# Deferred shared down products, last routers in one run, grouped last stage, expert word kept over the branch

## What is computed

```python
x = layernorm(x + attn(x))              # 16 heads, sqrt-distance bias; 2048 tokens of 256
xf = x.reshape(2048, 256)
scores = sigmoid(xf @ gate_w.T)         # 32 experts in 8 groups, the 4 best groups, the 6 best experts of those
w, idx = top6(mask_groups(scores)); w = w / w.sum() * 2.5
y = sum over the 6 picks: w * ((silu(xf @ w11[e].T) * (xf @ w33[e].T)) @ w22[e].T)
shared = (silu(xf @ sw1.T) * (xf @ sw3.T)) @ sw2.T
out = layernorm(x + y + shared)
```

## Time and profile before

| | us |
|---|---|
| median of 3 runs (lowest, highest) | 565.51 (562.99, 566.81) |
| the profiled execution | 565.8 |
| its span in the trace | 564.0 |
| busy of that span: PE, DVE, ACT, POOL | 459.8, 378.2, 321.9, 226.4 |

### The profile page before, as it was taken

The page is one execution under the profiler, slowest core; times in us unless marked ns, Lnnn a source line. Parts: engine busy times, 40 slices in busy tenths (PEclk is TensorE's granted clock), DMA queues, the critical chain, the costliest instruction groups (busy, mean ns, idle before and its releaser), DMA issues.

```text
span 564.0 us, 12967 instructions
## 1 busy us (share of the span) xinstructions
PE 459.8 (82%) x3190; PEld 377.7 (67%) x3191; DVE 378.2 (67%) x1745; ACT 321.9 (57%) x1093; POOL 226.4 (40%) x244
## 2 busy tenths in 40 slices
PE   4366779797968787767997999999999999992972
PEld 3254557575756555534556999898989898991761
DVE  4036385969697878974636677776767777772696
ACT  1059698878888979814102555555555555552133
POOL 0000000070716253477550657656566666563000
PEclk9669898889999989989999999999999999997897
DMA  4569659896978833289953555545455555523992
GB/s 130 125 221 269 153 139 267 228 273 164 242 170 234 203 103 102 77 307 416 416 198 82 168 153 166 160 145 168 139 154 158 156 160 158 143 63 121 420 409 95
DMA packets 67996, 107.92 MB, mean 191 GB/s; under 512 B 9189, under 2 KB 55018, under 8 KB 66416
## 3 DMA queue, kind: packets, MB, share of 16 engines
q1 hardware_dynamic: 54016, 75.15, 46.5%
q0 software_dynamic: 10752, 26.13, 14.0%
q10 hardware_dynamic: 3184, 6.13, 2.9%
HBM read 64.03 MB, written 43.33 MB: 190 GB/s over the span
## 4 chain that ended last, share of the span: by engine, by line
PE 55%; DVE 19%; DMA 10%; ACT 8%; issue 5%; SPq 2%; DVEq 0%; POOLq 0%; ACTq 0%; POOL 0%
PE bank L698 21%; PE bank L707 11%; DVE s_neg L980 5%; PE bank L688 5%; PE bank L637 5%; ACT probs L800 5%; DMA k_scratch<-k_lo 3%; PE bank L478 3%; DMA k_pack<-k_scratch 3%; PE bank L646 2%; PE bank L541 2%; ACT pT L811 2%; DMA xt<-xT 1%; DMA x1T_all<-x1T 1%; DVE ey_all L1339 1%
## 5 line engine op out<-in xcount | busy, mean ns | idle before, releaser
L1383 POOL DMA_INDIRECT routed<-rows,position x96 | 93.5, 974 | 194.5 <-DVE position L1144 166.9
L1393 POOL DMA_INDIRECT expert_out<-ey_all,out_row x128 | 130.1, 1017 | 93.4 <-issue 64.0
L800 ACT ACTIVATE probs<-s_neg,m_neg 128x128 f32<-128x128 f32 (+1 forms) x256 | 114.1, 450 | 38.1 <-DVE m_neg L980 37.9
L980 DVE CUSTOM_DVE_ANT_0 s_neg<-bank,bias_sb 128x128 f32<-128x128 f32 (+1 forms) x256 | 79.6, 351 | 54.7 <-PE bank L510 53.5
L898 ACT ACTIVATE eg<-bank 128x128 f32<-128x128 f32 x128 | 35.6, 278 | 88.9 <-PE bank L698 88.3
L707 PE MATMUL bank<-expert_w,ea 128*128 x256 | 78.8, 390 | 1.7 <-DVE ea L1296 0.6
L698 PEld LDWEIGHTS bank<-xgT,xn 128*128 128x128 f32 x512 | 66.5, 191 | 9.2 <-issue 5.6
L698 PE MATMUL bank<-xgT,xn 128*128 128x128 f32 x512 | 68.1, 276 | 3.6 <-issue 3.0
L510 PE MATMUL bank<-k_pack,q_pack 128*128 128x256 f32 (+1 forms) x128 | 58.3, 464 | 15.2 <-DMA k_pack<-k_scratch 12.6
L905 ACT ACTIVATE ey_all<-bank,pick 128x256 f32<-128x256 f32 x128 | 60.0, 469 | 1.8 <-DVE out_row L1309 1.5
L811 ACT ACTIVATE pT<-bank 128x512 f32<-128x512 f32 x96 | 55.8, 583 | 0.0
(11 more groups left out here) (160 smaller groups left out, 812.2 us busy)
## 6 DMA issues: line engine op xcount, KB each, us to landing
xg<-routed SPq DMA_DIRECT2D x128, 137.5 KB, 2.1
expert_w<-expert_out SPq DMA_DIRECT2D x16, 768.0 KB, 14.4
expert_w<-expert_weights SPq DMA_DIRECT2D x9, 1024.0 KB, 17.7
q_pack<-q_scratch SPq DMA_DIRECT2D x32, 256.0 KB, 5.0
routed<-empty SPq DMA_DIRECT2D x8, 550.0 KB, 12.8
k_pack<-k_scratch SPq DMA_DIRECT2D x16, 256.0 KB, 7.1
expert_w<-expert_weights ACTq DMA_DIRECT2D x3, 1024.0 KB, 13.5
xt<-xT SPq DMA_DIRECT2D x9, 256.0 KB, 7.8
```

What stands on the lines that cost most here:

```text
L800: act.activation(probs[g % 2][qb][:, 2 * pair + r, :], s_neg[u][:, r, 0:n], ACT.Exp, bias=m_neg[:, u, r:r + 1], scale=-1.0, accum_out=row_ ...
L980: dve.tensor_tensor_reduce(out=s_neg[u][:, r, 0:n], in0=SCORES[u][:, n * r:n * r + n], in1=bias_sb[:, REP * g + 2 * pair + r, SEQ - n:SEQ] ...
L1383: pool.indirect_dma_start(routed, bass.IndirectOffsetOnAxis(ap=position[b % ROW_BUFS][:, t, j:j + 1], axis=0), rows[b % ROW_BUFS][:, t, :] ...
L1393: pool.indirect_dma_start(expert_out, bass.IndirectOffsetOnAxis(ap=out_row[:, k:k + 1], axis=0), ey[k], None, bounds_check=TOKENS * TOPK - ...
```

## The change

The tiles of the shared down product are split in two. Eight (`SH_NOW`) are done in the transition as before. The other eight (`SH_LAST`) are done after the slot loop, straight into the eight PSUM banks, together with their `x_sum` tile; for this `sh_a` keeps all four blocks. The last stage works in groups of 4, 4, 4, 2 and 2 tiles: ten tiles are summed by TensorE and six by VectorE, and the small steps (root, polish, scale) are done once per group. In the transition the pieces of the routers of batches 6 and 7 stand in one run on VectorE, between them the layer norm of batch 7 and little else; TensorE does `shared_up` of the first block ahead of `ranks` of batch 6. The copies of batch 7 (`keep_x1`) go out from ScalarE's queue, ahead of its `gate_exps`, and not from SP's. SP waits for the tables first, reads two of them, and only then waits for the scatters. In the slot loop TensorE reads a word of `packed_tab` one slot after its first use before, and carries it over the loop's branch in a register (`word_back`). Several tiles take the place of others (`xgT` in `x1T`, `ey` in `rows`, `y_three` in `xg`).

```diff
...
-F_STATS = 9
 F_DEEP = 4
+F_GROUPS = ((0, 4), (4, 8), (8, 12), (12, 14), (14, 16))
+F_SUMMED = (0, 2, 4, 5, 7, 9, 10, 12, 13, 15)
+F_ADDED = tuple(t for t in range(TILES) if t not in F_SUMMED)
+SH_LAST = F_SUMMED[:8]
+SH_NOW = tuple(t for t in range(TILES) if t not in SH_LAST)
...
-        sh_a = [sb(f"sh_a{m}", [P, 512]) for m in range(2)]
+        sh_a = sb("sh_a", [P, 4, 2, 512])
...
-        xgT = [sb(f"xgT{i}", [P, KC, P], F32, late) for i in range(4)]
+        xg_all = sb("xg_all", [P, UNROLL, ROW], F32, late)
...
+        xgT = [x1T_flat[i // 2][:, DIM * (i % 2):DIM * (i % 2) + DIM].rearrange("p (c t) -> p c t", c=KC)
+               for i in range(4)]
...
-        ey_all = sb("ey_all", [P, UNROLL * DIM], F32, late)
-        ey = [ey_all[:, DIM * k:DIM * k + DIM] for k in range(UNROLL)]
+        ey = [rows[k // 2][:, k % 2, 0:DIM] for k in range(UNROLL)]
...
+        def f_source(t):
+            if t in F_SUMMED:
+                return bank[F_SUMMED.index(t) % 8][:, 0:DIM]
+            return f_resid[F_ADDED.index(t) % F_DEEP]
...
             load_weights(sp, 0)
             load_weights(sp, 1)
-            keep_x1(BATCH - 1, 1)
             load_weights(sp, 2)
             sp.wait_ge(pads_written, 16 * (BATCH + 1))
+            sp.wait_ge(fin_step, FIN_STEPS + 3)
+            def row_of(s):
+                return sp.value_load(slot_tab[0:1, bass.ds(s, 1)], min_val=0, max_val=EXPERTS * REGION)
+            early_rows = [row_of(k) for k in range(2)]
             for i in range(2):
                 sp.wait_ge(scattered[i], 16 * 2 * TOPK * BATCH // 2)
-            sp.wait_ge(fin_step, FIN_STEPS + 3)
...
             def load_slot(s, k, turn):
-                at = sp.value_load(slot_tab[0:1, bass.ds(s, 1)], min_val=0, max_val=EXPERTS * REGION)
+                at = early_rows[k] if turn is None and k < len(early_rows) else row_of(s)
                 if turn is not None:
                     sp.wait_ge(ey_ready[k], turn)
-                sp.dma_start(xg[k][:], routed[bass.ds(at, P), :]).then_inc(rows_loaded[k], 16)
...
             def shared_down(tb):
                 pe.wait_ge(sh_act, 2 * tb + 2)
-                for t in range(4):
-                    need(pe, sh_added, 4 * tb + t - 1)
-                    for m in range(2):
-                        last = pe.matmul(DOWN[t % 2][:, 0:DIM], sh_a[m][:, P * t:P * t + P],
-                                         sw2_sb[:, m, :], start=(m == 0), stop=(m == 1))
-                    last.then_inc(sh_down, 1)
+                for t in SH_NOW:
+                    if t // 4 == tb:
+                        n = SH_NOW.index(t)
+                        need(pe, sh_added, n - 1)
+                        down_tile(t, DOWN[n % 2][:, 0:DIM], True).then_inc(sh_down, 1)
...
             last_b = BATCH - 1
             values(last_b, 1, 1)
             project_out(last_b, 1)
-            ranks(last_b - 1, 0)
             shared_up(0, 0)
             shared_up(0, 1)
+            ranks(last_b - 1, 0)
             turn_x1(last_b, 1)
+            gate(last_b, 1)
             shared_up(1, 0)
-            gate(last_b, 1)
-            shared_down(0)
             shared_up(1, 1)
             ranks(last_b, 1)
             shared_up(2, 0)
...
             shared_up(2, 1)
-            shared_down(1)
+            shared_down(0)
+            shared_up(3, 0)
...
-            shared_up(3, 0)
             shared_up(3, 1)
+            shared_down(1)
             shared_down(2)
             shared_down(3)
             pe.wait_ge(fin_step, FIN_STEPS + 3)
-            pe.wait_ge(sh_added, TILES)
+            pe.wait_ge(sh_added, len(SH_NOW))
...
             def step(k, turn):
                 if k == 0 and turn.opens:
                     held.clear()
+                    if not turn.first:
+                        held["word"] = pe.snap(word_back, min_val=0, max_val=EXPERTS ** PACKED - 1)
                 if k == 0 and isinstance(turn.turn, int) and turn.turn < W_GROUPS - 1:
                     pe.wait_ge(late_loaded[turn.turn], 16 * W_PARTS)
-                now = None
                 if turn.exists(k, 0):
-                    now = held.pop("next") if "next" in held else expert_of(turn, k)
                     gate_up(k, turn)
-                following = turn if k < UNROLL - 1 and turn.slot is None else turn.next
-                if following is not None and turn.exists(k, 1):
-                    held["next"] = expert_of(following, (k + 1) % UNROLL)
+                if turn.exists(k, -1):
+                    if (k - 1) % PACKED == 0:
+                        held["word"] = experts_of(turn.turn * (UNROLL // PACKED) + (k - 1) // PACKED)
+                    last = expert_in(held["word"], k - 1)
                 if turn.exists(k, 2):
                     turn_rows(k, turn, 2)
                 if turn.exists(k, -1):
-                    last = held.get("last")
-                    if last is None:
-                        last = expert_in(experts_of(turn.turn * (UNROLL // PACKED) - 1), k - 1)
                     down(k, turn, last)
-                held["last"] = now
+                if k == UNROLL - 1 and turn.slot is None and turn.next is None:
+                    pe.reg_mov(word_back, held["word"])
...
+            for i in (0, 1, 6, 7, 2, 3, 4, 5):
+                t = SH_LAST[i]
+                if i == 2:
+                    for k in range(UNROLL - 4, UNROLL):
+                        pe.wait_ge(ey_ready[k], SLOTS // UNROLL)
+                down_tile(t, f_source(t), False)
+                pe.matmul(f_source(t), ident, x_sum[:, t, :], start=False, stop=False)
+            for n, t in enumerate(F_SUMMED):
+                to = f_source(t)
+                if n >= 8:
+                    pe.wait_ge(f_done, F_SUMMED[n - 8] + 1)
+                    pe.matmul(to, ident, x_sum[:, t, :], start=True, stop=False)
                 pe.wait_ge(rows_loaded[t % UNROLL], y_in(t))
-                need(pe, f_done, 2 * (p - F_DEEP + 1))
                 for j in range(TOPK):
-                    pe.matmul(to, ident, rows_y[:, t, DIM * j:DIM * j + DIM], start=(j == 0), stop=False)
-                pe.matmul(to, ident, x_sum[:, t, :], start=False, stop=True).then_inc(f_summed, 1)
+                    last = pe.matmul(to, ident, rows_y[:, t, DIM * j:DIM * j + DIM], start=False,
+                                     stop=(j == TOPK - 1))
+                last.then_inc(f_summed, 1)
...
             shared_silu(0, 0)
             shared_silu(0, 1)
             copy_x1t(last_b, 1, last_b // 2)
-            shared_silu(1, 0)
+            act.wait_ge(x1t_copied, BATCH)
+            act.dma_start(x1T_all[:, :, last_b * SEQ:BATCH * SEQ], x1T[1][:]).then_inc(x1_kept[1], 16)
+            act.dma_start(x_sum[:, 2 * last_b:2 * BATCH, :], x1[last_b % ROW_BUFS]).then_inc(x1_kept[1], 16)
             gate_exps(last_b)
             load_weights(act, W_GROUPS - 1)
-            shared_silu(1, 1)
-            for tb in (2, 3):
+            for tb in (1, 2, 3):
                 for m in range(2):
                     shared_silu(tb, m)
...
+            def final_apply(g):
+                act.wait_ge(f_fin, 5 * g + 5)
+                for i, t in enumerate(range(*F_GROUPS[g])):
+                    pair, at = t // 2, t // 2 % F_DEEP
+                    need(act, out_stored[at], 16 * (pair // F_DEEP))
+                    act.activation(f_out[at][:, t % 2, :], f_source(t), ACT.Identity,
+                                   scale=f_small[:, g % 2, 6, i:i + 1],
+                                   bias=f_small[:, g % 2, 7, i:i + 1]).then_inc(f_done, 1)
+                    if t % 2 == 1:
+                        act.wait_ge(f_done, t + 1)
+                        act.dma_start(out_t[t - 1:t + 1].rearrange("t p d -> p t d"), f_out[at]
+                                      ).then_inc(out_stored[at], 16)
...
+            for g, (a, z) in enumerate(F_GROUPS):
+                cols = f_small[:, g % 2, :, 0:z - a]
+                act.wait_ge(f_stat, f_stats_by(g))
+                act.activation(cols[:, 1, :], cols[:, 0, :], ACT.Ln).then_inc(f_root, 1)
+                act.wait_ge(f_root, 2 * g + 1)
+                act.activation(cols[:, 2, :], cols[:, 1, :], ACT.Exp, scale=-0.5).then_inc(f_root, 1)
+                if g > 0:
+                    final_apply(g - 1)
+            final_apply(len(F_GROUPS) - 1)
...
-                need(dve, sh_down, 4 * tb)
-                dve.tensor_tensor(sh_a[m][:], T_BANK[m][:], sh_g[m][:], ALU.mult).then_inc(sh_act, 1)
+                dve.tensor_tensor(sh_a[:, tb, m, :], T_BANK[m][:], sh_g[m][:], ALU.mult).then_inc(sh_act, 1)
...
             b = BATCH - 1
+            router_piece(b - 1, 0, 0)
             norm(b, 1, 1)
-            for part in range(4):
-                router(b - 1, 0, part)
+            for piece in range(1, 6):
+                router_piece(b - 1, 0, piece)
             ln_stats(b, 1, b // 2)
             ln_moments(b)
+            for piece in range(6, 10):
```

(51 more changed lines are left out.)

91 lines of the change are left out of this document (31 added, 60 removed).

## The result

The changed kernel took 550.08 us (median of 4 runs, 545.41 to 553.8) against 564.5 us (562.99 to 566.81) beside it: ratio 0.9702, 95% interval 0.9658 to 0.9747. The ratio leaves out the run of 553.8 us, which counts as slow (over 1.5% above the fastest), so it isn't the quotient of the two medians. A second measurement on another chip gave 548.12 against 565.43, ratio 0.9701 (0.9645 to 0.9758). Forecast: 550.0, between 545 and 557, faster.

A forecast was written before the change was run, and what follows sets the result against it. TensorE was taken to bound the loop, with scatters and TensorE's shared products setting its start; 564.0 - 10.1 + 1.7 - 4.7 - 2.7 = 548.2 us of span, with 1.8 around it 550.0, range 545 to 557.

The forecast's parts named there:

- What bounds the kernel: Loop start: scatters with row loads and TensorE's shared products end close together; relieving TensorE alone gains 5.6 us at most.
- Which part does it: Transition: deferring eight down tiles takes 7.4 us from TensorE, the new order brings scatters sooner; gain 10.1 us.
- Router and scatters: Transition: batch 7's `position` comes at about 265 us, so GpSimd needn't wait and issues its last scatter at 286.5.
- The lag: Last scatter's issue to SP's first row load: 3.98 us, less 0.6 for the table read moved ahead of the wait.
- rival 2: Scatters fall 2.6 us behind beside two weight queues; loop starts at 294.6, time 552.6 us; chance 0.12.
- The copies: Transition: batch 7's copies, issued 18 us before `shared_up(3, 0)` needs them, cost nothing.
- The clock: Loop start: after 6 us idle TensorE restarts at about half clock, costing 1.7 us; bounds 0 and 1.7.
- The branch: Slot loop: taking both table reads out of the gap at the branch gains 4.7 us; bounds 1.8 and 6.1.
- Rival 1: Slot loop: the branch itself keeps its price, gain only 1.8 us, time 552.9 us; chance 0.12.
- The last stage: After the loop: row transfer sets the floor, the last store comes 2.7 us sooner; bounds 0 and 4.5.
- rival 3: The last stage gains nothing; time 552.7 us; chance 0.09.
- rival 4: Last stage: TensorE's clock falls to 1.2 GHz throughout, making its added work slower; time 586.6 us; chance 0.04.

The follow-up runs named there:

- experiment 4: Changed kernel with order of routers and shared products as before and no down products deferred; rest kept: 560.73 us, ratio 0.9900.
- experiment 3: Changed kernel with the order of routers and shared products as before, eight down products still deferred: 547.74 us, ratio 0.9718.
- experiment 2: Changed kernel with all sixteen shared down products done in the transition, nothing deferred, new order kept: 544.27 us, ratio 0.9677.
- experiment 7: Changed kernel with the last 3 MB of weights sent by ScalarE behind the first two slots' copies in the loop: 548.48 us, ratio 0.9715.
- experiment 5: Changed kernel with fourteen products that nothing reads added on TensorE behind the last shared product, ahead of the loop: 546.37 us, ratio 0.9720.
- experiment 8: Changed kernel with the copies of batch 7 issued by SP between its weight transfers, not by ScalarE: 547.0 us, ratio 0.9722.
- experiment 1: Changed kernel with TensorE's two table reads returned to where the kernel before has them, at the loop's branch: 553.16 us, ratio 0.9837.
- experiment 10: Changed kernel with the last 3 MB of weights sent from SP behind its first eight row loads, four down products deferred: 557.37 us, ratio 0.9875.

## Why the prediction was right, point by point

- **What bounds the kernel.** It named two chains that end close together, TensorE's products and the scatters, and put 5.6 us on relieving TensorE alone. The runs bear out the picture and not that bound: the deferral alone took the transition from 61.87 (experiment 4) to 54.46 (experiment 3), 7.4 us, since it brings `position` 2.9 us sooner as well. The two chains aren't independent, because `shared_add` stood among the pieces of the router.
- **Which part does it.** Here the working was wrong without hurting the sum. It gave TensorE's earlier end to the deferral and the earlier scatters to the order. Experiments 2 to 4 show that the order alone brings both, and that the deferral adds nothing (transition 53.55 without it, 53.33 with it).
- **Router and scatters.** `position` of batch 7 was forecast 24.8 us behind the first scatter of batch 5 (265 - 240.25); it came at 24.0. The last scatter was forecast at 46.25 and issued at 46.12. The last `shared_add` was forecast to end at 45.8 (286 - 240.25); the products ended at 46.3 and the add at 46.8. These steps hold.
- **The lag: the term that was mis-sized.** Forecast 3.4 us, measured 4.99; that is the whole 1.6 us by which the transition falls short. Two sizes in it were wrong, in opposite directions. The weights were put at nothing, by "the weights are through by about 275", the argument against rival 2. They ended at about 290. From 256 to 284 us the DMA engines moved 0.41 to 0.42 MB per us in all, and 12 transfers of 1 MB (12.6 MB) with the scatters' 36 x 0.141 = 5.1 MB need 17.7 / 0.42 = 42 us at that rate, from some 248 us to 290. That sum could have been made beforehand. Before's own trace had the answer too: SP's queue, which has only weights left there, still moves 0.54 MB behind 284 us (first line below, DMA view of 284 to 292). The other size is the table read ahead of the wait, put at 0.6 us. Before reads the table from 293.4 us on, when the scatters have landed, and issues the first load at 294.42; after reads at 281.5 (second and third line). In experiment 4, where as in before the weights are through when the last scatter is issued, the lag is 2.72 and not 3.98: the new order on SP is worth 1.3 us (no run changes that order by itself). Against that lag the weights cost after 4.99 - 2.72 = 2.3 us, and experiment 7 shows that cause by taking them away (lag 2.73). So rival 2 came true beside the forecast, at 2.3 us and not 2.6, and 0.7 us of it came back on SP (1.3 and not 0.6).

```profile
q1 hardware_dynamic: 82, 0.54, 16.3%
...
L447 SPq TENSOR_LOAD <-slot_tab x128: 263/276/514, 293.4 to 500.6; - x128
...
L462 SPq TENSOR_LOAD <-slot_tab x128: 262/276/578, 281.5 to 491.2; - x128
```

  The rule of the Trainium skill that each DMA engine takes turns between the queues that have work (DMA: Bandwidth & Descriptors, "Queues, rings and completion order") agrees with the shares: 0.071 MB per us for the scatters beside two weight queues, 0.111 beside one.
- **The copies.** Forecast to cost nothing, 18 us ahead of their use; they came after some 20 and held TensorE for 1.3 us. That was hidden, since TensorE then had 7 us to spare ahead of the loop.
- **The clock.** Charged at 1.7 us, measured 1.5 (experiment 5). The price isn't fixed: the half clock lasted from 3.2 to some 6 us behind the same gap.
- **The branch.** Forecast -4.7. The runs whose loop starts at full clock have 205.14, 204.88, 205.03 and 204.88 (experiments 2, 3, 4, 8) and 204.46 (experiment 5) where before has 209.56: -4.4 to -5.1. Rival 1 falls. By the Trainium skill's rule (Runtime: NRT & Kernel Launch, "Instruction fetch mechanics") a stall that came from fetching the branch's target would have stayed with the branch; here 4.0 us in 80 slots went and came with the two reads (experiment 1). The 0.2 us that was left for the branch is still there, ahead of `down`: 0.9 us in five.
- **The last stage.** Forecast -2.7, measured -2.64. The rows arrive as before: the last sum starts 34.8 us after the first load of expert rows in after and 34.9 in before. What is shorter is the end behind it, forecast at 7.5 us (551.11 to 558.6) and measured at 7.3. Rivals 3 and 4 fall; the granted clock of the last stage was 0.97.
- **The number itself.** 564.0 - 8.57 - 3.61 - 2.64 = 549.2, with attention as in before, against 548.2 forecast. The profiled 552.0 has 2.8 us more of attention in it. The stages' sum was missed by 1.0 to 1.8 us, and the four runs spread over 8.4 us; that the median came within 0.1 us of 550.0 is luck.

## What to carry to other kernels

Where two chains end close together, price each part of a change with the other part absent, and only then together: here either of two parts brought 7 to 8 us, and the second 1 us or nothing. Before calling a stream of transfers "through by" some time, add up all bytes of all queues and divide by the rate that the DMA view shows; weights that are wanted late still push back the small transfers that are wanted now. And taking work from an engine that then stands idle can cost clock at its next start: leaving the work in the gap was as fast.

## What had not been expected of the hardware

The same program's attention took 243.06 us in one execution and 234.48 in another. VectorE and ScalarE were busy for the same time; TensorE was granted less clock in the longer one and was busy for longer. Windows from 180 to 220 us and the sums over attention, first the longer execution, then the shorter:

```profile
180.00:220.00 40.00, 32.57 (x251) 24.13 (x251) 33.81 (x188) 33.27 (x125) 14.12 (x17) 0.87 0.55 141
...
sum 243.06, PE 182.84 PEld 139.85 DVE 162.79 ACT 179.92 POOL 60.72; mean PE 26.12 PEld 19.98 DVE 23.26 ACT 25.70 POOL 8.67
```
```profile
180.00:220.00 40.00, 30.49 (x291) 22.63 (x291) 34.82 (x196) 36.26 (x138) 17.45 (x19) 1.00 0.53 146
...
sum 234.48, PE 170.23 PEld 130.25 DVE 162.78 ACT 179.61 POOL 60.89; mean PE 24.32 PEld 18.61 DVE 23.25 ACT 25.66 POOL 8.70
```

Those 8.6 us are about the spread of the four runs of after (545.41 to 553.8), and more than most of the edits here are worth. What makes the clock fall in one execution and not in the other was not tested. It fell in another place too: in experiment 10 TensorE was idle for 1.71 us ahead of the loop, and the granted clock was 0.72 over the stretch from 290 to 296 us; after 0.56 us (experiment 2) it stayed at 1.00.
